# First attention and first routing of a two-layer attention and expert network, as one unrolled stage

## The chip, the cores and the metric

One core of one Trainium2 chip. The time of a kernel is the device time of one execution in microseconds (us), and kernels are compared by the median of several runs. The profile is one more execution, recorded instruction by instruction.

## The reference, cut to what matters

The input x has 8 batches of T = 100 rows with 512 features; a context of 722 rows stands beside each batch. Two layers follow, each a cross-attention and a routed feed-forward network. All is float32. The change is in the first layer's attention and routing:

```python
q = (x @ q_w + q_b) ...; k = (context @ k_w + k_b) ...; v = (context @ v_w + v_b)   # 16 heads of 32
att = einsum('bhtd,bhsd->bhts', q, k) / sqrt(32)
att = softmax(where(tril, att, -inf))          # so only context rows 0..99 count
x   = x + einsum(att, v) @ o_w + o_b           # q from layernorm(x); then the feed-forward network,
u   = layernorm(x)                             # whose input is normalised twice:
xn  = layernorm(u) * gamma + beta
probs = softmax(xn @ Wg.T + bg); tp, ti = top_k(probs, 2); tp /= sum(tp) + 1e-8
y   = sum over the two chosen of 8 experts of tp * (gelu(xn @ W1[e].T + b1[e]) @ W2[e].T + b2[e])
x   = x + u + y
```

The second layer has an attention of 16 heads of 64 over 822 keys, and gated experts, routed in the same way.

## The kernel before, in words

`build` (L2082) runs stages one after another; `end_stage` (L96) clears the semaphores and holds all engines at a barrier between them. The stages: `attention_0` (L144), `route` (L553), `experts` of layer 0 (L770), `combine` of layer 0 (L1100), `project` (L1258), `attend` (L1508, the second attention, which also routes each batch as it goes, by `route_stats` to `route_slot`, L1891 to L1930, and ends with `passes`), `experts` and `combine` of layer 1. In each stage every engine has its own list of instructions, and semaphores, counted up and waited for, order them; each engine executes its list strictly in order.

**attention_0** works batch by batch. Its middle batches are a hardware loop of two batches per turn (`over_batches`), with a head and a tail written beside it. For one batch n, TensorE (PE) does in this order: `projections` (q and k as 16 fp32 products of 100 columns each, L290 and L300; v as a split product, L269), `turn_probabilities` of batch n-1 (L331), half of `scores(n)` (L315), `attended(n-1)` (L342), the other half, the transposes of the next x (L278), `output(n-1)` (L269). A split product writes each float32 factor as a rounded high part and a low part in the type F32R and adds three products per chunk of 128, so 12 products of 512 columns. For the scores the keys of four heads lie in a block-diagonal tile kD, which DVE fills with four adds of the bias (L410), and one product of 400 columns gives four heads at once. DVE then adds the mask from SBUF (L441), takes the maximum (L446), and ACT takes 16 exponentials with a sum each (L516); DVE divides P by the sums (L453). ACT copies the transposed P (L524). POOL writes zeros over the DRAM tensors slot_rows and slot_outs, 47 DMAs of 512 KB (L255), at the start.

**route** does all 8 batches at once: normalised rows (L662), their transposes (L636), logits (L643), a softmax, twice the best expert, and counts, from which DVE computes for each row the slots of its two experts and the table of passes (L689 to L747).

**experts** (layer 0): POOL scatters the rows to their slots with 16 indirect DMAs (L894) while SP loads the first two chunks of weights (L862); then SP loads 256 rows at a time (L854) and each of the 8 passes does one expert's two layers with split products (L945, L962). The weights are rounded by ACT (`high`, L1049) and subtracted by DVE (`low`, L982). For layer 1 the rows are scattered and the first weights rounded within `attend`.

**combine** gathers each row's two expert outputs by 16 indirect DMAs on POOL (L1144), and adds them with their weights through products with diagonals (L1156 to L1166).

## Time and profile before

| | us |
|---|---|
| median of 3 runs (1834.54 to 1837.36) | 1837.31 |
| the profiled execution, its own time | 1834.92 |
| its span, first to last instruction | 1833.3 |
| PE busy | 1645.1 (90%) |
| DVE busy | 1090.2 (59%) |
| ACT busy | 773.4 (42%) |
| POOL busy | 148.7 (8%) |
| TensorE's mean granted clock | 0.941 of full speed |

Busy is the time in which an engine executes something; waits and the issuing of DMAs are not counted. A share is an average over stages that have different limits, so each stage has to be read by itself. PEld is TensorE's loading of the stationary factor, which goes on beside its products. SPq and POOLq are the queues on which DMAs are issued. "xN" counts instructions (an fp32 product leaves two records); the text in brackets at the end of a line is the time that the engine stood idle before it, and what ended the wait.

### The profile page before, as it was taken

Reading aid. Unit: us, or ns where it says so; the run is one execution under the profiler, and the core shown is the slowest. Engines: PE = TensorE matmul, PEld = TensorE weight load, DVE = VectorE, ACT = ScalarE, POOL = GpSimd, SP = SyncE. Lnnn points to the kernel's source line nnn. Section 1 sums busy time; section 2 is a strip of 40 time slices with the busy share of each in tenths; the row PEclk is TensorE's granted clock in tenths of the full one; section 3 lists DMA queues with packets and bytes.
Section 4 is the critical chain, followed back from the end, with each engine's and each line's share of the span. In section 5 each row is a group of like instructions: output and inputs, shape, how many; then the busy total and the mean of one; then the engine's idle time right before and its main releaser. Section 6 shows DMA issues by size and latency. Waiting matters only on the chain. (4 is left out here: it accounts for less than half of the span.)

```text
span 1833.3 us, 31319 instructions
## 1 busy us (share of the span) xinstructions
PE 1645.1 (90%) x11708; PEld 1393.8 (76%) x11708; DVE 1090.2 (59%) x1887; ACT 773.4 (42%) x1469; POOL 148.7 (8%) x201
## 2 busy tenths in 40 slices
PE   5997439999999869979999999999999849999984
PEld 5785439999999639868787878778787549999981
DVE  5765536666666653326565656556565447667665
ACT  2454135555555422225354544435453324454440
POOL 6000230000000030110000000000000000000004
PEclk9998569999999979989999999999999879999996
DMA  8900075556555453340104133140102036556534
GB/s 306 395 10 1 11 251 206 205 205 205 204 205 205 158 160 120 122 143 23 49 20 147 41 125 129 37 146 22 57 23 88 11 127 218 205 192 228 206 124 118
DMA packets 86850, 249.69 MB, mean 136 GB/s; under 512 B 33256, under 2 KB 39784, under 8 KB 71404
## 3 DMA queue, kind: packets, MB, share of 16 engines
q1 hardware_dynamic: 68412, 175.72, 28.6%
q0 software_dynamic: 18352, 72.77, 11.4%
q8 instruction: 60, 0.98, 0.2%
q14 instruction: 26, 0.21, 0.0%
HBM read 197.39 MB, written 67.83 MB: 145 GB/s over the span
## 5 line engine op out<-in xcount | busy, mean ns | idle before, releaser
L1687 PE MATMUL banks<-a_ch,a_wm 128*128 128x362 f32 (+1 forms) x1024 | 286.0, 341 | 9.8 <-DVE a_cl L1848 9.8
L982 DVE TENSOR_TENSOR e_lo<-e_raw,e_hi 128x2048 fp32r<-128x2048 f32 x100 | 229.0, 2290 | 107.8 <-ACT e_hi L1049 107.8
L945 PE MATMUL banks<-e_xh,e_hi 128*128 128x256 f32 x768 | 218.0, 284 | 4.1 <-DVE e_xl L998 4.1
L945 PE MATMUL banks<-e_xh,e_lo 128*128 128x256 f32 x768 | 218.4, 284 | 0.0
L945 PE MATMUL banks<-e_xl,e_hi 128*128 128x256 f32 x768 | 218.3, 284 | 0.0
L1049 ACT CAST e_hi<-e_raw 128x2048 fp32r<-128x2048 f32 x100 | 190.4, 1904 | 51.6 <-PE banks L962 28.7
L1687 PEld LDWEIGHTS banks<-a_ch,a_wm 128*128 128x128 f32 x1024 | 186.2, 190 | 11.7 <-DVE a_cl L1848 11.2
L1687 PE MATMUL banks<-a_cl,a_wm 128*128 128x362 f32 (+1 forms) x512 | 168.9, 330 | 0.0
L1861 DVE TENSOR_REDUCE a_nmax<-banks 100x1 f32<-100x822 f32 x128 | 123.6, 1007 | 70.1 <-PE banks L1721 69.9
L945 PEld LDWEIGHTS banks<-e_xh,e_hi 128*128 128x128 f32 x768 | 147.8, 192 | 10.3 <-issue 4.5
L962 PE MATMUL banks<-e_hi,e_hh 128*128 128x512 f32 x384 | 152.7, 398 | 0.0
L945 PEld LDWEIGHTS banks<-e_xl,e_hi 128*128 128x128 f32 x768 | 147.9, 193 | 5.3
L962 PE MATMUL banks<-e_lo,e_hh 128*128 128x512 f32 x384 | 151.1, 394 | 0.0
L962 PE MATMUL banks<-e_hi,e_hl 128*128 128x512 f32 x384 | 149.7, 390 | 0.0
L945 PEld LDWEIGHTS banks<-e_xh,e_lo 128*128 128x128 f32 x768 | 147.8, 193 | 0.0
L2020 ACT ACTIVATE a_P<-banks,a_nmax 100x822 f32<-100x822 f32 x128 | 120.7, 954 | 3.5 <-DVE a_nmax L1861 3.4
L1732 PEld LDWEIGHTS banks<-ident,a_P 100*128 100x128 f32 (+2 forms) x896 | 82.2, 138 | 34.0 <-issue 31.7
L1085 ACT ACTIVATE e_hf<-banks,e_b 128x256 f32<-128x256 f32 x128 | 59.6, 472 | 113.4 <-PE banks L945 112.4
L1732 PE MATMUL banks<-ident,a_P 100*128 100x100 f32 (+2 forms) x896 | 101.9, 254 | 3.0 <-ACT a_PT L2028 3.0
L1721 PE MATMUL banks<-a_kT,a_q 64*100 64x512 f32 (+1 forms) x512 | 104.2, 526 | 0.0
L945 PE MATMUL banks<-e_xh,a_wm 128*128 128x256 f32 x512 | 95.1, 286 | 9.1 <-DVE e_hf L1013 5.8
L1687 PEld LDWEIGHTS banks<-a_cl,a_wm 128*128 128x128 f32 x512 | 98.1, 192 | 0.0
(292 smaller groups left out, 3042.3 us busy)
## 6 DMA issues: line engine op xcount, KB each, us to landing
e_raw<-wout SPq DMA_DIRECT2D x50, 1024.0 KB, 4.9
e_raw<-w SPq DMA_DIRECT2D x34, 1024.0 KB, 4.9
e_raw<-wgate SPq DMA_DIRECT2D x17, 1024.0 KB, 5.9
e_raw<-wup SPq DMA_DIRECT2D x17, 1024.0 KB, 4.9
slot_rows<-a_zero POOLq DMA_DIRECT2D x33, 512.0 KB, 17.2
a_craw<-ctxT SPq DMA_DIRECT2D x32, 361.0 KB, 4.2
e_xs<-slot_rows SPq DMA_DIRECT2D x18, 512.0 KB
slot_outs<-e_y POOLq DMA_DIRECT2D x16, 512.0 KB, 3.2
```

The source lines that it names most:

```text
L945: mm = nc.tensor.matmul(ps[:, bank, 0:CAP], w[:, cc, cut], x[:, cc, :], start=t == 0, stop=t == len(terms) - 1)
L962: mm = nc.tensor.matmul(ps[:, 4 + s, :], h[q % 4][:, cut], w[:, q % 4, :], start=q == 0 and t == 0, stop=q == NB - 1 and t == 2)
L982: nc.vector.tensor_tensor(lo[g % 2][i], raw[q % RAW][:], hi[g % 2][i].bitcast(F32), ALU.subtract)\
L1049: nc.scalar.copy(hi[g % 2][i], raw[q % RAW][:]).then_inc(hi_done, 1)
L1085: nc.scalar.activation(hf[kb % 4][:], ps[:, kb % 4, 0:CAP], ACT.Gelu, bias=b1[:, bass.ds(e * NB + kb, 1)]).then_inc(f_done, 1)
L1687: mm = nc.tensor.matmul(ps[:, 6 + half, 0:wide], w[:, cc, cut], x[:, cc, start:start + wide], start=cc == 0 and t == 0, stop=cc == DC - 1 ...
L1721: mm = nc.tensor.matmul(ps[0:T, 2 * two + f, 0:wide], q[s][r, :], kT[s][r, first:first + wide], start=True, stop=True)
L1732: mm = nc.tensor.transpose(ps[0:size, 4 + n // 5, T * (n % 5):T * (n % 5) + T], P[(2 * m + two) % 4][:, first:first + size], k.ident[0:T, ...
L1861: nc.vector.tensor_reduce(nmax[:, h:h + 1], two_banks(2 * two)[0:T, 0:KEYS], AX, ALU.max, negate=True)\
L2020: nc.scalar.activation(P[h % 4][:], two_banks(2 * two)[0:T, 0:KEYS], ACT.Exp, bias=nmax[:, h:h + 1], accum_out=sums[:, h:h + 1]).then_inc( ...
```

## The change

`attention_0` and `route` are replaced by one stage, `front`, whose 8 batches are written out one after another on every engine. Its parts:

- **Projection.** q and k are computed for two batches at once, 16 products of 200 columns for each of q and k; one such block stands in each of the batches 0 to 5.
- **Scores.** kD goes. The mask is put into PSUM by a product (identity times mask, F32R, one per bank), and 16 products with 32 contraction rows each, in four row groups with a bank each, are added onto it. DVE takes the maximum straight from PSUM; ACT takes the exponentials from PSUM, without sums.
- **Sums.** After the attended products, 16 products of the transposed P with ones give the sums in the layout of y; DVE takes the reciprocal and multiplies y. P is not divided.
- **Biases.** v_b goes through o_w once (a product with v_b spread over columns) and is added to o_b; POOL adds the sum to x of each batch. gamma and beta go into Wg and into a bias of the logits.
- **Routing per batch**, interleaved with the attention of later batches, with the operations of the second layer's routing (class `RouteTiles`, shared by both). Slots are spaced by SPAN = 1024 per expert, as in layer 1. The scatters are issued by POOL from batch 5 on. The zero writes are issued in four parts, in batches 0 to 3.
- **First expert weights** (three chunks loaded, two of them rounded) come in at the end of `front`, into tiles that held q_w, k_w, v_w and o_w.
- **combine** of layer 0 computes the two weights itself from the logits (softmax with two activations of ACT and ten small operations of DVE), as the softmax is gone from the routing.
- **Both layers** write the experts' outputs compactly (slot_outs, row j*256) and gather them through a second table `out_slot`, which `passes` computes with five more small operations; in `attend` the four DMAs that copied zeros over outs1 go, and the choice of both experts stands in one DVE step instead of two.

The diff, cut to its core (`...` marks what is left out):

```diff
+def front(k, ahead0):
...
             def _(sp):
+                x(0)
+                x(1)
+                sp.dma_start(qb[:], a["q_b"]).then_inc(qkb_in, 16)
+                sp.dma_start(kb[:], a["k_b"]).then_inc(qkb_in, 16)
+                weights("q")
+                context(0)
+                weights("k")
+                x(2)
+                weights("v")
+                x(3)
+                x(4)
+                sp.dma_start(vb[:], a["v_b"]).then_inc(c_in, 16)
+                sp.dma_start(ob[:], a["o_b"].partition_broadcast(T)).then_inc(c_in, 16)
+                sp.dma_start(wg[:], a["Wg0"].rearrange("(c p) e -> p c e", p=128)).then_inc(g_in, 16)
+                sp.dma_start(gam[:], a["gam0"]).then_inc(g_in, 16)
+                sp.dma_start(bet[:], a["bet0"]).then_inc(g_in, 16)
+                sp.dma_start(bg[:], a["bg0"].partition_broadcast(T)).then_inc(g_in, 16)
+                weights("o")
+                context(1)
...
             def _(pool):
+                pool.wait_ge(obs, 1)
+                per = -(-len(ZERO_ROWS) // ZERO_CYCLES)
+                for b in range(B):
+                    if b >= 1:
+                        route_root(b - 1)
...
+                    if b + 1 < B:
+                        add_bias(b + 1)
+                    if b < ZERO_CYCLES:
+                        for dst, n in ZERO_ROWS[per * b:per * (b + 1)]:
...
+                    if b == 5:
+                        pool.wait_ge(zeroed, 16 * len(ZERO_ROWS))
+                    if b >= 5:
+                        scatter(2 * (b - 5))
+                        scatter(2 * (b - 5) + 1)
+                route_root(B - 1)
+                scatter(B - 2)
+                scatter(B - 1)
+                pool.wait_ge(scattered, 32 * B)
...
             def _(pe):
+                def project_pair(g, which, ranked=0):
...
+                    for half in range(2):
+                        if half == 1:
+                            after(pe, rkc, ranked)
+                        for mo in (2 * half, 2 * half + 1):
+                            for cc in range(DC):
+                                o = 2 * T * (mo % 2)
+                                mm = nc.tensor.matmul(ps[:, 6 + half, o:o + 2 * T],
+                                                      w[which][:, cc, 128 * mo:128 * mo + 128], src[g % 2][:, cc, :],
+                                                      start=cc == 0, stop=cc == DC - 1)
...
+                def scores(b):
...
+                    for q in range(4):
+                        nc.tensor.matmul(ps[0:T, q, 0:4 * T], ident_r[:], mask_r[:].rearrange("p f t -> p (f t)"),
+                                         start=True, stop=False)
+                    for f in range(4):
+                        for q in range(4):
+                            rows_ = slice(HD0 * q, HD0 * q + HD0)
+                            mm = nc.tensor.matmul(ps[0:T, q, T * f:T * f + T], qT[g % 2][rows_, f, cut],
+                                                  kT[g % 2][rows_, f, cut], start=False, stop=f == 3)
...
+                def attended(b):
...
+                    for f in range(4):
+                        for q in range(4):
+                            mm = nc.tensor.matmul(ps[HD0 * q:HD0 * q + HD0, 5, T * f:T * f + T],
+                                                  ones[0:T, 0:HD0], PT[:, 4 * q + f, :], start=True, stop=True)
...
+                pe.wait_ge(pjs, 2)
+                project_pair(0, "k")
+                for b in range(B):
+                    scores(b)
+                    values(b)
...
+                    if b >= 2:
+                        route_logits(b - 2)
+                    if b >= 1:
+                        output(b - 1)
+                    if b >= 2:
+                        route_rank(b - 2)
+                    if block_at(b):
...
+                        project_pair(*block_at(b), ranked=b - 1)
+                    if b + 3 < B:
...
+                        turn_x(b + 3, 5)
+                    turn_probabilities(b)
+                    if b >= 1:
+                        route_turn(b - 1)
+                    attended(b)
+                route_logits(B - 2)
+                output(B - 1)
+                route_rank(B - 2)
+                route_turn(B - 1)
+                route_logits(B - 1)
+                route_rank(B - 1)
...
             def _(dve):
+                input_stats(0)
+                input_stats(1)
+                normalise_rows(0)
+                normalise_rows(1)
+                input_stats(2)
+                dve.wait_ge(g_in, 64)
...
+                normalise_rows(2)
+                projected(0, "q")
...
+                context_low(0)
+                projected(0, "k")
+                weights_low(1, wv, "v")
+                input_stats(3)
+                input_stats(4)
+                for b in range(B):
+                    if b >= 1:
+                        scaled(b - 1)
+                    highest(b)
+                    if b >= 2:
+                        route_best(b - 2)
+                    if b == 0:
+                        dve.wait_ge(c_in, 32)
+                        nc.vector.tensor_copy(vb_wide[:], bc(vb[:], T)).then_inc(vbw, 1)
+                        weights_low(2, wo, "o")
+                        dve.wait_ge(obm, 1)
+                        nc.vector.tensor_tensor(ob[:], ob[:], ps[0:T, 5, :], ALU.add).then_inc(obs, 1)
+                    if b >= 1:
+                        add_output(b - 1)
+                    if b >= 2:
+                        route_slot(b - 2)
+                    if b + 3 < B:
+                        normalise_rows(b + 3)
+                    if block_at(b):
+                        projected(*block_at(b))
+                    if b % 2 == 0 and b // 2 + 1 < PAIRS:
+                        context_low(b // 2 + 1)
+                    if b + 5 < B:
+                        input_stats(b + 5)
+                    if b >= 1:
+                        route_rows(b - 1)
+                scaled(B - 1)
+                expert_weights_low(0)
+                route_best(B - 2)
+                add_output(B - 1)
+                route_slot(B - 2)
+                route_rows(B - 1)
+                expert_weights_low(1)
+                route_best(B - 1)
+                route_slot(B - 1)
+                r.passes(nc, own)
...
             def _(act):
+                def exponents(b):
+                    act.wait_ge(nm, b + 1)
+                    for q in range(4):
+                        for f in range(4):
+                            h = 4 * q + f
+                            ins = nc.scalar.activation(P[:, h, :], ps[0:T, q, T * f:T * f + T], ACT.Exp,
+                                                       bias=nms[b % 2][:, h:h + 1], scale=HD0 ** -0.5)
+                        ins.then_inc(e, 1)
...
+                for b in range(B):
+                    if b >= 1:
+                        attended_high(b - 1)
+                    exponents(b)
+                    values(b)
+                    if b == 0:
+                        weights_high(wo, "o")
+                    if b % 2 == 0 and b // 2 + 1 < PAIRS:
+                        context_high(b // 2 + 1)
+                    if b + 3 < B:
+                        turned_x(b + 3, 5)
+                    turned(b)
+                    if b >= 1:
+                        route_turned(b - 1)
+                expert_weights_high(0)
+                attended_high(B - 1)
+                expert_weights_high(1)
+                route_turned(B - 1)
...
 def combine(k, layer):
+                nc.vector.tensor_tensor(sm[:, 0, :], k.best[:, 1, :], k.best[:, 0, :], ALU.subtract).then_inc(dif, 1)
                 if layer == 0:
+                    nc.vector.tensor_tensor(ex[:], k.logits[:], bc(k.best[:, 0, :], E), ALU.subtract).then_inc(dif, 1)
+                    dve.wait_ge(wexp, 2)
+                    own.link(nc.vector.tensor_reduce(sm[:, 1, :], ex[:], AX, ALU.add))
+                    own.link(nc.vector.reciprocal(sm[:, 1, :], sm[:, 1, :]))
...
 def attend(k, s1, ahead1):
-                    if b < CLEAR:
-                        part = slice(CLEAR_ROWS * b, CLEAR_ROWS * (b + 1))
-                        pool.dma_start(k.outs1[part].rearrange("(p s) d -> p (s d)", p=128),
-                                       k.outs0[0:CLEAR_ROWS].rearrange("(p s) d -> p (s d)", p=128))\
-                            .then_inc(cleared, 16)
...
                     if m == LOGITS_AT and b >= 1:
-                        route_best(b - 1, 0)
-                    if m == SECOND_AT and b >= 1:
-                        route_best(b - 1, 1)
+                        route_best(b - 1)
```

## Rows read from the trace of the kernel before

**Rows 1.** Windows of the stages; us, busy time and instructions by engine, granted clock, DMA.

```profile
67.60:86.20 18.60, 18.36 (x149) 14.69 (x148) 13.29 (x19) 8.61 (x40) 0.00 (x0) 1.00 1.03 408
...
164.20:189.20 25.00, 12.31 (x73) 8.44 (x71) 10.52 (x12) 8.35 (x37) 0.00 (x0) 0.66 0.00 1
...
190.00:224.00 34.00, 17.28 (x100) 16.72 (x100) 22.94 (x98) 5.68 (x17) 6.10 (x14) 0.50 0.02 1
...
224.00:260.40 36.40, 1.97 (x8) 1.57 (x8) 7.17 (x7) 7.80 (x8) 18.58 (x16) 0.50 0.70 245
```

**Rows 2.** TensorE in order of time, 48 to 60 us: start, us, operation.

```profile
48.83 1.51 PE L315 MATMUL banks<-a_kD,a_qT 128*100 128x400 f32 x4
...
50.27 0.89 PE L342 MATMUL banks<-a_PT,a_v 100*32 100x100 f32 x32
...
52.81 0.45 PE L269 MATMUL banks<-a_wo_hi,a_yhi 128*100 128x512 f32 x1
...
55.41 0.39 PE L269 MATMUL banks<-a_wo_hi,a_ylo 128*100 128x512 f32 x1
...
55.64 3.71 PE L290 MATMUL banks<-a_xT,a_q 128*128 128x100 f32 x32
```

**Rows 3.** Groups of instructions of DVE and ACT, four steady batches, 67.6 to 142 us.

```profile
L441 DVE TENSOR_TENSOR a_P<-banks,a_mask 100x1600 f32<-100x1600 f32 x4 | 7.3, 1825 | 1.6 <-PE banks L315 1.6
...
L446 DVE TENSOR_REDUCE a_nm<-a_P 100x16 f32<-100x1600 f32 x4 | 7.2, 1809 | 0.0
...
L403 DVE TENSOR_TENSOR a_qT<-banks,a_qb 128x400 f32<-128x400 f32 x4 | 2.3, 574 | 0.9 <-PE banks L290 0.9
...
L516 ACT ACTIVATE a_P<-a_P,a_nm 100x100 f32<-100x100 f32 x64 | 23.2, 364 | 21.1 <-DVE a_nm L447 21.1
```

**Rows 4.** TensorE in order of time in the second attention.

```profile
1351.63 0.87 PE L1782 MATMUL banks<-r_wg,r_xT 128*100 128x8 f32 x8
...
1352.43 1.63 PE L1721 MATMUL banks<-a_kT,a_q 64*100 64x512 f32 x8
```

**Rows 5.** Head: SP's queue, DVE and TensorE in order of time, 0 to 35 us.

```profile
14.04 2.01 SPq L229 DMA_DIRECT2D a_ob<-o_b  x1
...
24.76 2.29 DVE L421 TENSOR_TENSOR a_wv_lo<-a_v,a_wv_hi 128x2048 fp32r<-128x2048 f32 x1
...
29.96 2.85 PE L315 MATMUL banks<-a_kD,a_qT 128*100 128x400 f32 x8
```

**Rows 6.** A gap on TensorE, and windows behind it and in the last batch.

```profile
35.35 5.44 PE L290 MATMUL banks<-a_xT,a_q 128*128 128x100 f32 x32 [2.19 <-DVE a_xT L398]
...
35.00:39.00 4.00, 3.65 (x20) 3.66 (x21) 3.96 (x4) 1.73 (x10) 4.00 (x9) 0.63 1.04 384
...
176.00:186.00 10.00, 8.51 (x57) 6.33 (x58) 0.78 (x2) 2.46 (x5) 0.00 (x0) 0.50 0.01 2
```

**Rows 7.** Start of the first experts: SP's queue and TensorE in order of time.

```profile
250.68 0.39 SPq L854 DMA_DIRECT2D e_xs<-slot_rows  x1
...
260.43 0.57 PE L945 MATMUL banks<-e_xh,e_hi 128*128 128x256 f32 x1 [4.15 <-DVE e_xl L998]
```

**Rows 8.** End of the second attention and start of the second experts: DVE, then TensorE.

```profile
1468.10 0.69 DVE L1883 TENSOR_TENSOR x_res<-x_res,banks 100x512 f32<-100x512 f32 x1 [4.91 <-PE banks L1764]
...
1476.86 0.17 DVE L1918 TENSOR_TENSOR r_sel<-r_onehot 100x8 f32<-100x8 f32 x1
...
1478.56 0.17 DVE L1928 CAST slot<-r_slotf 100x2 uint32<-100x2 f32 x1
...
1496.27 0.57 PE L945 MATMUL banks<-e_xh,a_wm 128*128 128x256 f32 x1 [3.29 <-DVE e_xl L998]
```

**Rows 9.** One batch of the second attention, as a window.

```profile
1123.00:1196.00 73.00, 72.94 (x604) 58.88 (x603) 43.08 (x85) 33.72 (x78) 3.18 (x4) 1.00 0.32 100
```

**Rows 10.** First combine: DVE, then TensorE, in order of time.

```profile
642.07 1.06 DVE L1191 COPY c_dT<-banks 108x400 f32<-108x400 f32 x2 [0.51 <-PE banks L1156]
...
654.81 1.07 PE L1164 MATMUL banks<-c_y,c_dg 100*100 100x512 f32 x2 [0.42 <-DMA c_y<-slot_outs,slot]
```

1168 lines of the change are left out of this document (501 added, 667 removed).

## The prediction, made before the changed kernel ran

> **What bounds the kernel now.** I read the stage windows first [rows 1]. The window 67.60:86.20 is one batch of the first attention: TensorE is busy 18.36 of 18.60 us at a granted clock of 1.00, so the steady batch is bound by TensorE and by no wait. The last batch (164.20:189.20) has 12.31 us of product in 25.0 us; the routing (190:224) keeps DVE busy 22.94 of 34 us and gives nobody else much to do; from 224 to 260.4 TensorE works 1.97 us. So 95 us stand between the last score product and the first expert product at 260.43 [rows 7], mostly in series. What comes after is packed already: the copies that the change drops from the second attention run while TensorE is busy 72.94 of 73 us [rows 9].
>
> So the sum is a date: when does the first product of expert pass 0 begin? It is 260.4 now. The eight passes, the projection, the second attention and its experts keep their work, so the kernel gains what this date gains, less what is added behind it.
>
> **TensorE's prices at full clock** [rows 2]. A split product of 12: 11 steps from 52.81 to 55.41, 0.236 each, 2.8. An fp32 matmul is two records: 0.116 each with 100 columns (3.71/32), where the weight load sets the pace, and 0.335 with 400 ((1.51-0.50)/3). For the paired projection (200 columns, 32 records) I take half of the 400-column price, 0.167: 5.35 per block, one block per batch for b=0 to 5, where 7.4 (3.71 twice) stood per batch. Ends: 0.116 (3.7) and a straight line between the two rows, 0.189 (6.0). That the stage is unrolled costs nothing: the second attention is too, and is full [rows 9]. The 16 attended products in four column groups cost 0.9; the product with ones is of the same form, so 1.75 for both. Logits 0.87 [rows 4], rank 0.45 by half of that, each set of four transposes 0.46, the 16 of P 2.0 with their copies.
>
> **The scores** are new: four F32R products of the mask (0.236*400/512, 0.75 in all), then 16 fp32 products with 32 rows in four row groups. By the 400-column record (0.335) one of 100 columns streams in 0.084: 2.7 for 32 if nothing overlaps. Column groups of the same size took 0.9 [rows 2], and two 64-row groups took 1.63 [rows 4] for two heads of 822 columns, 2.75 in series by the same price. I take 0.8, so 1.55 in all against 2.7 now; the other end is 3.45.
> The Trainium skill (TensorE: Matmul & The Clock Gate, Measured speedup vs the span model) has four row tiles at 3.07 times, not 4: by it the 16 products take 0.9 and a batch 0.1 more. The two-group row shows 1.7 times.
>
> **A batch of TensorE in the new stage**, b=2 to 4: 1.55+2.8+0.87+2.8+0.45+5.35+0.46+2.0+0.46+1.75 = 18.5, with semaphores 18.8. The projections save 2.05 and the scores 1.15, and ones and routing take 3.4 back: the steady batch does not get shorter, it takes the routing in. b=1 has no routing products (17.4), b=5 no transpose of x (18.2).
> DVE in such a batch [rows 3]: reciprocal, product and low part 3*0.57, reduce 1.81+0.17 (the mask add 1.82, the division of P of the same size and four copies of K go), route_best 12 small operations in 2.4 (from 1474.62 to the end of L1918 [rows 8]), add_output 0.69+0.69 [rows 8] and three small, 2.1, slots 0.8, x 0.54, two copies 1.15, low part of the context 1.0, statistics 1.1, route_rows 1.4: 14.2 of 18.8. On b=2 the rows come 0.5 late for route_turn: 19.2. ACT: 16 exponents at 0.36 each with the accumulator read [rows 3]; without it and from PSUM I take 0.33 (lower end 0.25), 5.3; the copies 4*0.5 (DVE takes 0.57 for as many columns [rows 3]).
> Batches 6 and 7 have no projection and hang on the chain: scores 1.55, y of the batch before and reduce to 4.5, exponents to 9.8, values 0.6, four copies with two turns 2, attended 1.75: 14.1. TensorE idles in them, and after an idle of 2.19 us before 35.35 the granted clock was 0.63 over the next 4 us [rows 6]; I add 1.4 to each: 15.5.
> b=1 to 7: 17.4+19.2+18.8+18.8+18.2+2*15.5 = 123.4.
>
> **The head, up to scores(1).** Now scores(0) start at 29.96 [rows 5]. x(0), x(1) and q_w go first, but DVE now waits for g_in before it normalises x(2) and copies Q: the 18th issue on SP's queue. The 17th ends at 16.05 now; four more small ones and their landing make it about 21. Then Q copied at 24, K projected by 30, scores(0) at 30.5: nothing gained. Behind them DVE does wv's low part 2.29 [rows 5], two statistics 2.2, reduce to 37; exponents to 42.5; ACT only then rounds wo (1.9), DVE subtracts (2.3) and adds the bias: 48; normalise(3), copies of K(1), transposes and their copies, attended: scores(1) at 54, where they are at 48.8 [rows 2]. In b=0 the serial chain of wo costs about 5 us. Range 47 to 58. The 47 zero writes move behind it, 12 in each of four batches, 6.5 us of POOL's queue, which has 10 us spare; scatters wait for them in b=5.
> T7, the end of attended(7): 54+123.4 = 177.4.
>
> **The tail.** y 2.4; output at half clock as in the last batch now (0.50 in 176:186 [rows 6]) 5.1, beside it DVE has an expert's low part 2.29 and route_best(6) 2.4; add_output 2.1; slot(6) 0.8; route_rows 0.6 (POOL's root beside it); transposes, copy, logits 2.6; the second low part holds DVE to 14.8; best 2.4, rank 0.9, slots 0.8: slots(7) at T7+19.2. The chain from the output's end to slots takes 1468.10 to 1478.73, 10.6, in the second attention [rows 8]; here it is 11.7 from T7+7.5, the rest being those low parts and batch 6.
> **From the last slots to the first product**: 1478.73 to 1496.27, 17.5 [rows 8]: two indirect writes, landing, the stage's end, rows of x, transposes, rounding. This layer scales xf, 0.8 more: 18.3. The longer table arithmetic (five operations, 1.0) ends before the writes land in both layers. SP's three small loads go beside TensorE's reading of the count; if not, 1.2. 16 writes in series, which hold SP's load until 250.68 now [rows 7], are down to two.
> Date: 177.4+19.2+18.3 = 214.9; gain 260.4-214.9 = 45.5.
>
> **Behind it.** combine(0) computes the weights itself: two ACT exponents and ten small operations, 4 to 5 us, before the diagonals. Now dT is ready at 643.1 while gathers still pace the last batches from 654.8 on [rows 10]; four batches of catching up in between hide all but 1; without that cover 5. The dropped copies (16 MB in the second attention): nothing, as a saturated TensorE covers them [rows 9]; bounds 0 and 1 gained. route_best in one piece there delays a DVE step by 1.3, under a slack of about that: 0 to 2 lost. One register load more on SP per pass of layer 0, one less on POOL: 0.
>
> The profiled execution spans 1833.3 (its time 1834.9), 2.4 under the median 1837.3. 1837.3-45.5+1 = **1793**.
>
> **Rivals.**
> 1. The row groups do not overlap: 1.9 per batch, 15 in all, since scores lie on the path in every batch: 1808. Against it: two groups do [rows 4]. 0.12.
> 2. The head is better than I think (g_in lands by 16, the wo chain hides), the projection is at its lower end (-1.65*6) and the exponents at theirs: 12 to 20 more gained, 1776. DMA shares were full at that time, which speaks against. 0.2.
> 3. DVE becomes the bound: 14.2 of 18.8 leaves 4.6; if the many waits between small operations and TensorE's in-order queue cost 2 more in each of seven batches, 1807. 0.15. The GPSIMD Engine Reference of the Trainium skill (Key points) speaks for it: GpSimd shares its SBUF interface with VectorE and is about half as fast elementwise, so POOL's new bias adds take 1.4 each by its figure (an estimate) and may slow DVE's two-input operations meanwhile. By it the sum is 2 to 3 higher. No row of before has POOL and DVE adding together.
> 4. Slower than before: the clock stays at its low level through the stage. The stage has 8*18 = 144 us of TensorE; at half clock it has 288. From a third of that work at low clock on, the 45 are gone; with half, 72 more, 1865. The place is the wait for the exponents, now once in every batch. For it: the low clock after 35 and in 176:186 [rows 6]; against it: for b=1 to 5 the queue has 14 us of products in front of that wait, against 9.8 of chain. 0.03.
> 5. The change does not do what it says, the routing of batches 0 to 5 waiting in fact for the end: +15, 1808. The order of the queues excludes nearly all of it. 0.02.
>
> **Numbers.** My forecast 0.48, rivals 0.12, 0.2, 0.15, 0.03, 0.02. Range 1774 to 1811: from rival 2 to rivals 1, 3 with a bit of both. Faster by over 0.2% (3.7 us, what a measurement of this kernel can tell from no change): 0.95; within 0.2%: 0.02; slower: 0.03.
>
> **What would show it.** First expert product near 215; scores(1) near 54, then steps of 18 to 19 with TensorE above 95% busy for b=1 to 5, 14 to 16 for the last two; the 16 score products within about 1 us; DVE under 15 us per batch; slots(7) about 19 after the last attended; 46 us per pass as now. It is wrong if a batch takes over 21 or under 16, if TensorE waits for DVE in the steady batches, if the head ends beyond 60, or if the second half of the kernel moves by more than 3 us.

## The result, and the profile after the change

The changed kernel takes 1818.37 us (median of 4 runs, 1817.51 to 1819.29) where the kernel before takes 1837.17 in the same comparison: ratio 0.9901, interval 0.9884 to 0.9918. It is faster by 18.8 us; 44 were forecast (1793, range 1774 to 1811). The profiled execution spans 1817.3 us, 16.0 less than before. Line numbers below are those of the changed kernel.

| | forecast | measured | late by |
|---|---|---|---|
| score products of batch 1 begin | 54 | 53.38 | -0.6 |
| from there to the end of attended(7) | 123.4 | 143.5 | 20.1 |
| from there to the last slots | 19.2 | 20.3 | 1.1 |
| last slots to first expert product | 18.3 | 22.9 | 4.6 |
| first expert product | 214.9 | 240.10 | 25.2 |

The date that the forecast is about moved by 20.3 us [rows 7], not 45.5. The first view of the kernel after is the windows of one steady batch, of the last two, of the tail, and of the stretch up to the first expert product [rows 1 for those of before].

```profile
core 0: us, PE busy (x) PEld busy (x) DVE busy (x) ACT busy (x) POOL busy (x), PEclk, DMA share, GB/s
93.79:114.50 20.71, 18.15 (x197) 15.29 (x193) 13.97 (x33) 7.54 (x24) 13.88 (x25) 1.00 0.97 365
156.02:176.40 20.38, 15.88 (x159) 12.03 (x157) 12.41 (x30) 7.24 (x23) 5.96 (x6) 0.80 0.14 39
176.40:196.90 20.50, 17.12 (x158) 12.53 (x157) 11.61 (x30) 8.94 (x24) 4.71 (x5) 0.75 0.16 44
196.90:217.30 20.40, 10.03 (x41) 7.78 (x40) 16.82 (x47) 2.91 (x3) 4.57 (x3) 0.58 0.08 22
217.30:240.10 22.80, 1.97 (x8) 1.57 (x9) 6.72 (x33) 4.04 (x6) 1.96 (x2) 0.50 0.42 150
```

TensorE's work in the steady batch is 18.15 us, where 18.5 were counted; the batch takes 20.71. So it is not the work that was misjudged but 2.56 us of waiting, 12% of the batch in an engine that was to be over 95% busy. TensorE in order of time in that batch (the last column in brackets is the idle time before the row and what ended it):

```profile
93.79 0.97 PE L483 MATMUL banks<-a_mask_r,a_ident_r 100*100 100x400 f32 x4
94.69 0.96 PE L488 MATMUL banks<-a_kT,a_qT 32*100 32x100 f32 x32
97.32 0.47 PE L441 MATMUL banks<-e_hi,a_ctxhi 128*100 128x512 f32 x1 [1.67 <-DVE a_y L669]
103.94 5.66 PE L466 MATMUL banks<-a_xT,e_raw 128*128 128x200 f32 x32
110.27 0.89 PE L517 MATMUL banks<-ident,a_P 100*100 100x100 f32 x8 [0.32 <-DVE a_qT L641]
111.49 0.92 PE L517 MATMUL banks<-ident,a_P 100*100 100x100 f32 x8 [0.33 <-ACT a_PT L804]
112.99 0.89 PE L531 MATMUL banks<-a_PT,a_v 100*32 100x100 f32 x32 [0.24 <-ACT a_PT L804]
113.70 0.87 PE L536 MATMUL banks<-a_PT,a_ones 100*32 100x100 f32 x32
114.50 0.97 PE L483 MATMUL banks<-a_mask_r,a_ident_r 100*100 100x400 f32 x4
```

1.67 + 0.32 + 0.33 + 0.24 is the whole of the 2.56. The first of them is the one that matters: the value products go to the bank of the attended rows, so they wait for a_y, made of them. What makes a_y late stands in VectorE's rows of the same batch:

```profile
94.00 2.66 DVE L667 RECIPROCAL a_rec<-banks 128x400 f32<-128x400 f32 x1 [1.55 <-PE banks L536]
96.69 0.57 DVE L669 TENSOR_TENSOR a_y<-banks,a_rec 128x400 f32<-128x400 f32 x1
97.86 0.57 DVE L672 TENSOR_TENSOR a_y_lo<-a_y,a_y_hi 128x400 fp32r<-128x400 f32 x1 [0.59 <-ACT a_y_hi L809]
98.35 1.82 DVE L657 TENSOR_REDUCE a_nm<-banks 100x16 f32<-100x1600 f32 x1
106.61 1.50 DVE L629 TENSOR_SCALAR a_xn<-x_res,a_mv,a_rs 100x512 f32<-100x512 f32 x1
```

The reciprocal of the 128x400 sums takes 2.66 us, 4.7 times the product of the same size below it. I had priced both at 0.57. At 0.57, a_y would be ready at about 95.2, before TensorE has done with the scores at 95.65.

VectorE's busy time in this batch is 13.97 us (the window above), as good as the forecast's 14.2, and so came true as a sign. That says nothing for the forecast: the reciprocal and the 1.50 us operation at 106.61 took 3.05 more than their 0.57 and 0.54, and batch 3 has neither the low part of a context nor the two statistics, 2.1 together, that the sum counted.

In batches 6 and 7 another wait comes up (the rows are of batch 6; batch 7 has the same 1.80): the transposes of P wait until VectorE has read the ranks (r_taken) from the bank that they share. TensorE's granted clock is low behind it, 0.80 and 0.75 over these two batches: 32 sum records that take 0.87 above are spread from 172.79 to 176.47.

```profile
166.10 0.53 PE L517 MATMUL banks<-ident,a_P 100*100 100x100 f32 x4
168.43 2.43 PE L517 MATMUL banks<-ident,a_P 100*100 100x100 f32 x12 [1.80 <-DVE r_taken L193]
171.45 1.56 PE L531 MATMUL banks<-a_PT,a_v 100*32 100x100 f32 x32
172.79 1.51 PE L536 MATMUL banks<-a_PT,a_ones 100*32 100x100 f32 x24
176.40 1.66 PE L483 MATMUL banks<-a_mask_r,a_ident_r 100*100 100x400 f32 x4
```

The end of the stage, first in order of time on POOL, SP's queue and TensorE [rows 7], then the drains of GpSimd at the end of the first stage (L318) and of the second attention (L1651): duration in ns three times, start in us.

```profile
218.79 0.98 POOL L402 DMA_INDIRECT slot_rows<-r_rows,slot  x1 [0.30 <-issue]
228.78 0.33 SPq L917 DMA_DIRECT2D e_b<-b  x1
230.32 0.38 SPq L930 DMA_DIRECT2D e_xs<-slot_rows  x1
240.10 0.57 PE L1005 MATMUL banks<-e_xh,e_hi 128*128 128x256 f32 x1 [4.21 <-DVE e_xl L1058]
```
```profile
L318 POOLq DRAIN  x1: 5213/5213/5213, 222.4 to 222.4; - x1
L1651 POOLq DRAIN  x1: 1359/1359/1359, 1467.7 to 1467.7; - x1
```

Between 222.2 and 228.7 no transfer runs and no engine is busy; 5.21 us of it are one DRAIN, an instruction that stands in every engine's queue at the end of a stage (GpSimd's is the long one).

**Behind the first stage.** The experts' eight passes take 45.9 us each, as before, and the end of the first combine's last gather keeps what the first stage gained (21.9 us earlier). The second attention loses: its first added output is 21.3 us earlier than before, its last [rows 8] only 16.65, and the period from one batch to the next is 81.0 us where it was 80.35. In the waits of six of its batches (us in total, times, longest) TensorE has a new one (at its weight load), and ACT's for the maxima has a longest of 1.3:

```profile
ACT a_P L2011 <- DVE a_nmax L1901: 8.8, 12, 1.3
PEld banks L1748 <- ACT a_kT L2006: 4.1, 6, 0.7
```

Before, the second of these is not there, and the first is

```profile
ACT a_P L2020 <- DVE a_nmax L1861: 2.8, 12, 0.3
```

### The profile page after: what moved, and what is told of

It reads as the page before. It is cut to its first block and busy times, and to the rows that moved or that the text cites. A ratio compares the mean times of both kernels' runs of the same rounds, so it can differ in the third digit from the quotient of the medians.

```text
span 1817.3 us, 31629 instructions
## 1 busy us (share of the span) xinstructions
PE 1644.4 (90%) x11976; PEld 1392.7 (77%) x11976; DVE 1080.6 (59%) x1968; ACT 764.2 (42%) x1348; POOL 156.2 (9%) x208
## 5 line engine op out<-in xcount | busy, mean ns | idle before, releaser
L1042 DVE TENSOR_TENSOR e_lo<-e_raw,e_hi 128x2048 fp32r<-128x2048 f32 x98 | 224.4, 2290 | 94.8 <-ACT e_hi L1106 94.8
L1106 ACT CAST e_hi<-e_raw 128x2048 fp32r<-128x2048 f32 x98 | 186.7, 1905 | 29.4 <-PE banks L1022 29.4
```

What stands on the lines that cost most here:

```text
L1042: nc.vector.tensor_tensor(lo[g % 2][i], raw[q % RAW][:], hi[g % 2][i].bitcast(F32), ALU.subtract)\
L1106: nc.scalar.copy(hi[g % 2][i], raw[q % RAW][:]).then_inc(hi_done, 1)
```

## Experiments

Each started from the changed kernel. A comparison puts a kernel beside the kernel before on one chip (medians 1835.3 to 1837.1). The changed kernel itself took 1818.37 us in the first comparison and 1814.77 and 1814.69 in two others (experiment 5), so differences under 4 us between kernels of different comparisons say nothing here. Ratios are to the kernel before. A step is the time from the first score product of one batch to that of the next.

**1. The reciprocal twice.**
```
-    nc.vector.reciprocal(rec, ps[:, 5, ...]).then_inc(yr, 1)
+    for n in range(2):
+        nc.vector.reciprocal(rec, ps[:, 5, ...]).then_inc(yr, 1)
+        dve.wait_ge(yr, 2 * b + n + 1)
```


> The reciprocal of the 128x400 sums is issued twice in each batch, the second over the first. Theory A (the y path through VectorE, sums product, reciprocal 2.66 us, product with it, then the value product, is on the path of every batch): each step from one batch's score products to the next grows by 2.7 us, from 20.75 to about 23.4, TensorE's wait for a_y before the value products grows from 1.66 to about 4.35 us; with the tail, eight such: the first expert product comes 19 to 21.5 us later (240.1 to about 260) and the time is about 1839. Rival B (VectorE has slack in a batch of 20.7 us with 14 of work, and TensorE would wait for something else anyway, the projection's copy or the probabilities): less than 1 us per batch, the time under 1826.

1848.28 us, 1.0062 (1.0044 to 1.0079): slower than the kernel before. VectorE and TensorE in batch 3:

```profile
103.87 5.35 DVE L668 RECIPROCAL a_rec<-banks 128x400 f32<-128x400 f32 x2 [1.55 <-PE banks L536]
109.89 0.75 PE L441 MATMUL banks<-e_hi,a_ctxhi 128*100 128x512 f32 x1 [4.36 <-DVE a_y L670]
```

The wait grew by what the second reciprocal takes, 2.7, and rival B fell. But the first expert product came 29.1 us later (269.22), not 21.5, and the time is 9 us over Theory A's 1839, as the steps grew by 3.0 to 5.2. The rest is the clock: the first value product behind the longer idle takes 0.75 us for 0.47, and in 80:85 and 85:90 the granted clock is 0.70 and 0.62. In batch 2 (78.09 to 103.67) TensorE is busy 20.35 us, where it was busy 18.29: 2.1 of its step's growth of 4.8, and the wait is the other 2.7. In this kernel an idle of over 4 us per batch costs itself and some products at the low clock.

**2. Sums first, banks exchanged.** The product with ones goes ahead of the attended products and has a semaphore of its own.
```
 def values(b):
-    pe.wait_ge(yn, b)
-    split_product(4, ...)
+    pe.wait_ge(yr, b)
+    split_product(5, ...)
 def output(b):  def turn_x(b + 3, ...):
-    bank 5
+    bank 4
```


> The product with ones goes ahead of the attended products, and the value products go to the bank of the sums (free when the reciprocal has read it) instead of the bank of the attended rows; the output product and the turned rows go to the other. Theory A: the reciprocal starts 0.8 us earlier beside the attended products and the value products no longer wait for the 0.57 us product behind it: TensorE's wait before them falls from 1.66 to about 0.3 us in batches 1 to 6, six times 1.36 = 8.2 us, and 0.8 in the tail: the time is about 1809. Rival B (the wait only moves to the turned probabilities, whose exponents and projection copies come no earlier): the steps stay at 20.7 less at most 0.4, the time 1815 or more.

1805.27 us, 0.9825 (0.9808 to 0.9841).

```profile
91.45 2.66 DVE L670 RECIPROCAL a_rec<-banks 128x400 f32<-128x400 f32 x1 [0.87 <-PE banks L532]
94.16 0.47 PE L442 MATMUL banks<-e_hi,a_ctxhi 128*100 128x512 f32 x1 [0.37 <-DVE a_rec L670]
```

The reciprocal now begins 0.48 us before the scores of batch 3 (91.93), where it began 0.21 behind them, and the wait is 0.37. The steps are 19.4. The first expert product comes at 226.97, 9 to 13 us sooner than in three executions of the changed kernel, and the time is 9.4 us under that kernel's in the other comparisons (experiment 5): Theory A.

**3. The banks alone.** The diff of experiment 2, with the order of the two products as in the change.

> Only the exchange of the banks: the value products wait for the reciprocal alone, the order of the two products is as in the change. Theory A (the gain of the sums first, 9.5 us beside the unchanged kernel's 1814.8, is the sum of 0.8 us by the order and 0.6 us by the bank in each batch): TensorE's wait before the value products falls from 1.66 to about 1.06 us, the steps from 20.7 to 20.1, the time is 1809 to 1811. Rival B (the order alone did it): the wait stays over 1.5 us and the time near 1815.

1806.95 us, 0.9836 (0.9821 to 0.9851). The wait before the values is 1.06 us, the steps 20.1: as Theory A says, bank and order each give their part of a step. The first expert product comes at 230.28, 3.3 us behind experiment 2's. The total is 2 us under the forecast and 1.7 above experiment 2, where 5 were to be expected; comparisons on different chips do not resolve that.

**4. Bank 3 for the turned probabilities of batches 6 and 7.**
```
-    if q == 1: after(pe, rkc, b - 1)
+    if q == 1 and block_at(b): after(pe, rkc, b - 1)
+    if q == 1 and not block_at(b): pe.wait_ge(e, 4 * b + 4)
-    transpose(ps[0:T, 6 + q % 2, ...])
+    transpose(ps[0:T, 6 if q % 2 == 0 else 7 if block_at(b) else 3, ...])
```


> In batches 6 and 7 alone (those with no projection) the second and fourth groups of turned probabilities go to bank 3, which is free once the exponents have read it, instead of bank 7, which VectorE must first have read the ranks from. Theory A1 (the wait of 1.80 us for the ranks is also what lets the clock fall): the wait goes but for about 0.4 us, twice 1.4, and the products now at the low clock (sums 3.68 and 3.61 for 0.87, attended 1.56, scores 3.3 for 1.9, the first values, the last output product 5.0 for 2.8) take their fast times, some 9 to 12 us more: the time is 1804 to 1807. Theory A2 (the clock falls all the same, these batches having less work for TensorE): only the two waits go, 2.8 us, the time is about 1815.5. Rival B (the exponents are as late): nothing, 1818.

1814.17 us, 0.9865 (0.9844 to 0.9886). The wait for the ranks is gone; next late is the wait for the routing rows:

```profile
175.07 0.56 PE L550 MATMUL banks<-ident,r_rows 100*128 100x100 f32 x4 [2.12 <-DVE r_rows L698]
```

A1 fell: step 6 is 17.96 here, but it is 17.8 and 17.5 in other executions of the changed kernel with the wait in place (next). Whether A2's 2.8 us are there stays open: the ratio is 4 us under the unchanged kernel's with intervals that overlap, while the trace has a new wait of much the size of the old one. One pair of executions hints at 2 us: from the scores of batch 1 to the first expert product it takes 172.8 us in experiment 2, and 170.8 in the kernel of experiment 12 that has this edit besides.

**5. The changed kernel again**, in two other comparisons.

> The changed kernel itself, unedited, beside the next three on the same chip. It is the yardstick for small differences: 1818.4 us again if a kernel with an unchanged first stage differs from another only by its edit. Of that stage I want to know whether the low clock of batches 6 and 7 (steps of 20.4 and 20.5 us) belongs to the program or falls elsewhere from one execution to the next, as a run with another edit alone, with a step of 17.69 in the same place, lets one suspect. Belongs to it: steps of 20.4 again. Falls by chance: a step of about 17.7 in one of them, and the times spread by some 3 us or more.

> The changed kernel itself beside both: 1815 to 1818 us; the six edits are then worth 29 to 33 us.

1814.77 (0.9888, 0.9871 to 0.9904) and 1814.69 (0.9885, 0.9869 to 0.9900): here the change is worth 20.5 and 21.8 us, where the first comparison had 18.8. Steps between score products, and the first expert product:

| execution | 1 | 2 | 3 | 4 | 5 | 6 | product |
|---|---|---|---|---|---|---|---|
| first profile | 19.6 | 20.8 | 20.7 | 20.7 | 20.8 | 20.4 | 240.10 |
| again | 19.6 | 22.4 | 20.7 | 20.7 | 20.7 | 17.8 | 239.31 |
| again (b) | 19.5 | 20.8 | 20.7 | 20.7 | 20.7 | 17.5 | 236.22 |

The same program has the low clock in different batches. The windows are batches 2 and 6 of the execution "again"; the mean granted clock is 0.92 and 0.91, where the first profile has 1.00 and 0.80.

```profile
74.46:96.87 22.41, 19.87 (x196) 16.25 (x192) 14.78 (x37) 8.37 (x25) 8.47 (x15) 0.92 0.79 318
159.03:176.83 17.80, 13.79 (x161) 10.65 (x157) 12.43 (x30) 7.12 (x23) 4.93 (x5) 0.91 0.08 21
```

So the 20.4 of batch 6 in the first profile is not the program's alone: 17.5 and 17.8 stand elsewhere, 16.4 in experiment 9, whose edit does not touch the batches, and the rest fell to it in that execution.

**6. Two steps for the choice in the second attention.**
```
     if m == LOGITS_AT and b >= 1:
-        route_best(b - 1)
+        route_best(b - 1, 0)
+    if m == SECOND_AT and b >= 1:
+        route_best(b - 1, 1)
```


> The choice of the two experts in the second attention goes back to two steps of its schedule (first choice at step 5, second at step 6), all else stays. Theory A (eleven linked VectorE operations in one step, 2.4 us, delay what the attention's next step needs of VectorE, 0.65 us per batch): the period from one batch's added output to the next goes from 81.0 back to 80.35 us, seven times 0.65 = 4.5 us, the time is about 1814. Rival B (the longer period comes from something else that the change did there, such as the copies to DRAM that are gone or the wider tiles): the period stays at 81.0 and the time within 1 us of 1818.4.

1809.25 us (runs from 1806.74 to 1816.25), 0.9856 (0.9827 to 0.9884), and a period of 80.4 us. TensorE's wait for a_kT is gone, and the row of the maxima is as before:

```profile
ACT a_P L2029 <- DVE a_nmax L1915: 2.8, 12, 0.3
```

Theory A is shown: the longer step delays the reduction, that ACT's exponents, and those ACT's copy of the keys. From the first added output to the last it takes 555.9 us for 560.4: 4.5 us less, as Theory A has it.

**7. The bias addition on VectorE**, in add_output, and taken from GpSimd.
```
+    nc.vector.tensor_tensor(xb, xb, ob[:], ALU.add).then_inc(obx, 1)
     dve.wait_ge(od, b + 1)
```

> The addition of the output bias goes from GpSimd back to VectorE, ahead of the addition of the output product. Theory A (VectorE is not what bounds a batch; GpSimd's 1.3 us addition stretches a VectorE operation beside it from 0.55 to 1.5 us, and that operation is not on the path either): the normalised rows take 0.54 us in every batch, the steps stay at 20.7 within 0.2 us, the time within 1.5 us of 1814.8. Rival B (VectorE bounds, or the stretched operation delays the projection's copy and so the turned probabilities): the steps move by 0.5 us or more, the time by 3 us or more, up if the added 0.69 us counts and down if the contention does.

1814.55 us, 0.9877 (0.9861 to 0.9894), the steps unchanged within 0.1 us. The normalised rows of batch 3, beside which POOL had been adding:

```profile
107.68 0.55 DVE L620 TENSOR_SCALAR a_xn<-x_res,a_mv,a_rs 100x512 f32<-100x512 f32 x1
```

0.55 for 1.50: the addition beside it stretched this operation, and the kernel lost nothing by that. As a test of whether VectorE bounds a batch the edit is weak, since it takes 0.95 us from VectorE and gives it 0.69. The rows of the change are better evidence: before the reciprocal of the next batch, at 114.71, VectorE stood idle for 3.27 us until TensorE's sums were there.

**8. The routing bias late in the head.**
```
 TensorE:
-    wait wgs; ones x wgb; turn_x(2, 5); project_pair(0, "k")
+    turn_x(2, 5); project_pair(0, "k"); wait wgs; ones x wgb
 VectorE:
-    wait g_in; wgg, wgb; normalise_rows(2); projected(0, "q"); lbias; context_low(0); projected(0, "k")
+    normalise_rows(2); projected(0, "q"); context_low(0); wait g_in; wgg, wgb; projected(0, "k"); lbias
```

> In the head, the product that makes the routing bias, and VectorE's work on the routing weights, go behind the first context projection. Theory A (in the order of the change TensorE stands 4.6 to 6.4 us for four small transfers that come last, while the key weights are there): the first score products come 3 to 5 us sooner, at about 28.5, and the time falls by 2 to 4 us, the weights of the values and of the output permitting. Rival B (the head is bound by the large weights, which come at the rate of the DMA): the first score products at 28.5 but the second ones still near 53, the time unchanged within 1 us.

1807.73 us, 0.9859 (0.9841 to 0.9877), 7.0 under experiment 5 on the same chip.

```profile
9.07 8.15 PE L466 MATMUL banks<-a_xT,e_raw 128*128 128x200 f32 x32 [0.98 <-DMA e_raw<-q_w]
18.14 5.68 PE L466 MATMUL banks<-a_ctx,e_raw 128*128 128x200 f32 x32 [0.34 <-DVE a_qT L641]
24.80 0.94 PE L483 MATMUL banks<-a_mask_r,a_ident_r 100*100 100x400 f32 x4 [0.35 <-DVE r_lbias L727]
```

The first scores come at 24.80 instead of 32 to 34, the second at 45.60: more than A asked for, as the key projection also runs at the full clock (5.68 us at a granted clock of 1.00, where it took 7.72 at 0.72 behind an idle of 4.56). The large weights were there.

**9. Forty semaphores more.**
```
+    spare = [k.sem(f"a0_spare{n}") for n in range(40)]
```

> Forty semaphores that nothing uses are added to the first stage, about 80 before; all of a stage are cleared at its end. Theory A (the 6.8 us from VectorE's last operation to the first instruction of the experts, for 3.6 behind the second attention with about 56, are the clearing, one by one, in front of the barrier): at the 0.1 us each that this pair gives, the gap grows by about 4 us and so does the time. Rival B (it is the scatters' landing and the first reads of the table): the gap stays at 6.8 us.

The gap is 7.05 us for 6.80, the clearing 0.675 us for 0.458. Theory A fell. The time was 1811.5 (two runs), within the spread of the changed kernel.

**10. The rows ahead of the small transfers.**
```
-    b1, gam, bet; ...; rows(0)
+    rows(0); b1, gam, bet
```

> The experts' first rows are asked for ahead of the three small transfers (bias, gamma, beta), which stand 1.5 us before them on the queue; nothing else changes. Theory A (from the end of the first stage to the first expert product everything is one chain): the first expert product comes 1.5 us sooner, the time falls by 1.5 us, to about 1813.3. Rival B (the rows are then early but gamma and beta late): no change, or up to 1 us slower.

1813.99 us, 0.9880 (0.9865 to 0.9896); last slots to first product 22.3 for 22.9. The rows' issue gained 0.6 of the 1.5: it comes 12.5 us behind the slots, where the first of the small transfers had come 11.6 behind them. In total nothing could be told.

**11. An early drain, and fewer writes.** The runs so far left the 5.21 us DRAIN. Listing the drains at the ends of the two attention stages of both kernels beside the DMAs that GpSimd issued in the stage gives one price. The kernel before:

```profile
L206 POOLq DRAIN  x1: 3903/3903/3903, 92.6 to 92.6; - x1
L1598 POOLq DRAIN  x1: 1686/1686/1686, 1484.1 to 1484.1; - x1
```

47 DMAs in the first (the clearing writes), 20 in the second; after the change 16 in the second attention (1.359) and 63 in the first stage (5.213): 0.083 to 0.085 us each. The stages between fit too: 24 DMAs in the kernel before's first experts (16 scatters, 8 outputs) and 8 after the change, which moved the scatters out:

```profile
L834 POOLq DRAIN  x2: 725/1380/2034, 634.9 to 1788.4; - x2
L913 POOLq DRAIN  x1: 721/721/721, 614.1 to 614.1; - x1
```

The combines do not fit: their 16 gathers would give 1.3 us, and the drains take 2.56 and 16.6.

```profile
L1127 POOLq DRAIN  x2: 2556/9590/16625, 646.4 to 1822.6; - x2
```

The longer one starts at 646.4, while ten of the 16 gathers are still to be issued, and ends 3.8 us behind the last. So the price holds where all has landed and GpSimd has no work of its own under way. Two kernels test it.
```
     pool.wait_ge(zeroed, 16 * len(ZERO_ROWS))
+    pool.drain()
```
```
-    pool.dma_start(dst[CAP * n:CAP * (n + 1)]..., zero[:])
+    pool.dma_start(dst[CAP * n:CAP * (n + m)]..., zero[:] broadcast m times)
```


> GpSimd drains once more in the first stage, behind its wait for the 47 clearing writes and ahead of the first scatter; nothing else changes. Theory A (a drain of GpSimd takes some 0.083 us for every DMA that it issued since the drain before): the early drain takes 3.9 us, where nothing waits for it, the one at the stage's end falls from 5.21 to 1.36 us, and the first expert product and the end come 3.85 us sooner: about 1811, against 1814.8 of the unchanged kernel beside a kernel before of 1835. Rival B (it waits for the scatters' last writes, or costs the same at the end of any stage of such length): it stays at 5.21 us, the time unchanged.

> The same bytes are cleared by 13 writes of up to 2 MB instead of 47 of 512 KB (each reads the zeros up to four times). Theory A (the drain goes by the number of DMAs): 29 of them, the drain at the end takes 2.4 us, 2.8 less, the time is about 1812. Rival B (it goes by bytes or descriptors): 5.2 us as before.

The early drain itself, then the drain at the stage's end with it, then that with 13 writes for 47:

```profile
L427 POOLq DRAIN  x1: 5906/5906/5906, 147.0 to 147.0; - x1
```
```profile
L318 POOLq DRAIN  x1: 1364/1364/1364, 218.4 to 218.4; - x1
```
```profile
L318 POOLq DRAIN  x1: 2437/2437/2437, 221.7 to 221.7; - x1
```

The two at the end are within 0.04 us of the rule: it goes by the number of DMAs issued since the last drain, not by bytes. The early one takes 5.91 us where Theory A had 3.9. It starts at 147.0 with a root and a bias addition of GpSimd, which end at 148.98; from there it takes 3.97. Last slots to first product: 18.9 and 20.1 us for 22.9, which is 4.0 and 2.8 less, where the shorter drains give 3.85 and 2.78. The times, 1812.13 (0.9877, 0.9860 to 0.9893) and 1813.59, are too near the unchanged kernel's ratio for the total alone to show it.

**12. Together.** Three edits are those of 2, 4 and 6; five have also 8 and 10; six also the early drain.

> The three edits of the runs before together: the sums first with the banks exchanged, bank 3 for the turned probabilities of batches 6 and 7, two steps for the choice in the second attention. Theory A (three separate places on the path): the sum of the three, 13 + 1 to 4 + 4.5 us below the changed kernel, about 1798. Rival B (they share what they gain, the first two above all, by the clock): 1803 or more.

> The three edits, the routing bias late in the head, and the experts' first rows ahead of their three small transfers. Theory A (five separate places on the path): 1796.2 less 7.0 less 1.5 = about 1788. Rival B (with the head shorter, the weights of values and output or the contexts come too late for batches 1 to 3): 1793 or more.

> The five edits and the early drain. Theory A: 1788.3 less 3.85 = 1784.5. Rival B (the early drain delays a root or a scatter that is on the path once the rest is short): 1787 or more.

> The kernel with five edits, beside the one with six on the same chip: the yardstick, about 1788 us.

> Theory A (nothing gives back what the shorter drain gains): 3 to 4 us below the kernel with five edits on the same chip. Rival B (the low clock, which falls in other places from one execution to the next, or the early drain gives it back): less than 1.5 us below.

| kernel | us | ratio (interval) |
|---|---|---|
| three edits | 1796.15 | 0.9792 (0.9775 to 0.9808) |
| five edits | 1788.32 | 0.9740 (0.9727 to 0.9754) |
| six edits | 1786.98 | 0.9737 (0.9721 to 0.9752) |
| five edits, one chip | 1790.86 | 0.9755 (0.9735 to 0.9774) |
| six edits, same chip | 1785.06 | 0.9722 (0.9708 to 0.9736) |
| changed kernel, same chip | 1814.69 | 0.9885 (0.9869 to 0.9900) |

The edits add up, as far as these times can tell. With all six the kernel is 29.6 us below the changed kernel and 51 below the kernel before. What the early drain adds to the five is not settled by the times: 1.3 us in the first pair, on two chips, which is rival B's 1787 by a hair, and 5.8 on one chip, by medians whose ranges overlap. The drains in the traces differ by 3.85.

## Why the prediction was wrong

The sign and the idea were right: the date of the first expert product sets the gain, what follows is packed, and the gain of that date arrived behind the experts. The sum was wrong by 25 us in that date, and by 3 behind it. Of the 20.1 us between the first scores of batch 1 and the last attended product, batches 1 to 5 make 10.2, and batches 6 and 7 make 9.9.

- **Head, right in the sum.** 54 against 53.38, and partly by luck: scores(0) came at 32.48 for 30.5, and the way from there to scores(1) took 20.9 us for 23.5, on which the sixteen exponents are, priced at 5.3 and measured at 3.87 in batch 3. From "nothing gained" in front of the first scores I concluded that nothing was to be had; the wait for g_in, which I described, was worth 7 us by a change of order (experiment 8). I costed it and did not ask which other work could stand in it.
- **"Reciprocal, product and low part 3*0.57": the step that failed.** I took the price of one VectorE operation for another of the same size. It is 2.66 us, and it stands between two products of TensorE. That is a wait of 1.60 to 1.67 us in each of batches 1 to 6 (batch 7 waited 0.24, with its scores at the low clock), 10 us, half of the 20.1, and a longer chain in the tail, where y takes 4.6 us for 2.4. Experiments 1 to 3 show it from both sides. Only small reciprocals (100x1) run before the change, so its price should have been a range, and rival 3 (VectorE late) would have got the weight. The Trainium skill (VectorE: DVE Perf Modes, First, the fixed hardware budget) says that the reciprocal is an iterative divide with a repeat count of 8, and that an ADD needs one of the pipe's 8 slices. It gives no time for the reciprocal. The row agrees in kind: 6.6 ns per column for 1.4.
- **TensorE's prices, right.** 18.15 for 18.5; a projection 5.66 for 5.35, the sixteen score products 0.96 for 0.8 with the mask 0.97 for 0.75. Rival 1 is out. (That ones and routing "take 3.4 back" does not follow from their own terms, which give 2.6; the sum of 18.5 does not use it.) I let 0.3 for the semaphores; the three small waits at the turned probabilities take 0.9.
- **"Batches 6 and 7: 14.1 + 1.4 = 15.5": a wait missing, and the clock too small.** The turned probabilities share bank 7 with the ranks, and VectorE reads those only after add_output: 1.80 us each, which I had left out of the chain; the exponents, 1.4 less than priced, hid part of it. Taking the wait out uncovered the next, for the routing rows (experiment 4). With it the step is 16.4 to 17.8 in executions that have the clock there; the 20.4 and 20.5 of the first profile also have the low clock, which other executions have elsewhere or less of. It made some 4 us in each there, for the 1.4 that I had added (20.4 less the 16.4).
- **"From the last slots to the first product: 18.3": 4.6 short.** I carried the 17.5 over from the second layer, whose stage issues 20 DMAs from GpSimd. The new stage issues 63, and its drain takes 3.5 us more than that one's 1.69. In the kernel before, the drain over the 47 clearing writes ran at 92.6, beside the attention, and so was in none of my sums: the change moved it onto the path. Of the other 1.1 the three small transfers ahead of the rows, which the forecast priced at 1.2 and then at nothing, make 0.6 (experiment 10). Part of the drain came back: the 16 scatters left the experts' stage, whose drain fell from 2.03 to 0.72 us (experiment 11).
- **"route_best in one piece: 0 to 2 lost": 4.6.** The slack of about 1.3 that I gave the step was not there; the reduction behind it is needed at once. The condition for "wrong" on this point (the second half moves by over 3 us) was met, and so was the one on TensorE waiting for VectorE. The sign "DVE under 15 us per batch" came true (13.97) all the same: a busy time does not show that one operation stands where TensorE waits for it.
- **combine(0): 1 lost: not seen.** The last gather ends 21.9 us earlier, at a gain of 20.3 at the first product; the shorter drain in front of the gathers is 1.3 of the difference.
- **Rival 4** (low clock throughout) stayed out: 1.00 over the steady batches of the first profile.
- **GpSimd's additions beside VectorE**, the second half of rival 3. They take 1.26 to 1.49 us each. The estimate by the GPSIMD Engine Reference of the Trainium skill (Key points) was 1.4. They slow VectorE (1.50 us for 0.55), and that was worth nothing (experiment 7).

Left open: what of the low clock belongs to which batch, as it differs between executions; and the 0.9 us in front of the rows that the new place of the small transfers did not bring.

## What to carry to other kernels

Price an operation by its own kind: a reciprocal is not an add of the same size, and where no row shows it, its cost is a range with a rival of its own. When work is moved into a stage, ask what the stage's end then waits for, its drains included, as these stood under other work before. Read a busy time as no more than a sum: an engine can be within its forecast and still hold up another in every batch. Where an engine stands idle beside a bank that two uses share, an exchange of banks and an order that makes the long operand first can be worth more than the work saved.

## What the runs showed of the hardware that was not expected

- A DRAIN of GpSimd takes 0.083 to 0.09 us per DMA that it issued since the drain before, though all of them had landed: 0.72 us for 8, 1.36 for 16, 1.69 for 20, 2.03 for 24, 2.44 for 29, 3.90 for 47, 5.21 for 63. Where GpSimd still has work or DMAs under way, it takes longer (5.91 for 47, 16.6 for 16).
- VectorE's reciprocal of 128x400 from PSUM takes 2.66 us, in every one of the batches, and twice it takes 5.35.
- A 100x512 VectorE operation with scalars from SBUF takes 0.55 us alone and 1.50 beside GpSimd's addition of the same size.
- The low granted clock falls in other batches from one execution of the same program to the next; a step of 20.7 us became 22.4 by it.
